# Three of four transposed attention tiles copied by ScalarE, with every engine's turn order redrawn

## What is computed

```python
x = x + L0_gnn(ln(x), adj)      # g0: three GRU steps over the adjacency
x = x + L0_ffn(ln(x))           # f0: eight experts, two chosen per node
x = x + L1_gnn(ln(x), adj)      # g1: one masked softmax attention
x = x + L1_ffn(ln(x))           # f1: attention over 64 slices, 8 heads
x = x + L2_gnn(ln(x), adj)      # g2: mean over neighbours
x = x + L2_ffn(ln(x))           # f2: a state-space block
x = x + L3_gnn(ln(x), adj)      # g3: two masked 4-head attention layers
x = x + L3_ffn(ln(x))           # f3: the upper half of the rows gets an FFN
```

```python
scores = einsum('bqhd,bkhd->bhqk', q, k) * scale
scores = where(adj_mask, scores, NEG_INF)
out = einsum('bhqk,bkhd->bqhd', softmax(scores), v)
```

## Time and profile before

| | us |
|---|---|
| three runs, median (lowest to highest) | 3333.42 (3329.63 to 3334.25) |
| the profiled execution | 3333.91 |
| its span, first to last instruction | 3332.1 |
| half 0, from its first transposes | 161.4 |
| a middle half | 198.9 |
| half 16 | 172.1 |

### The profile page before, as it was taken

One profiled execution on the slowest core, in us unless ns is written; L12 is line 12 of the kernel. 1 busy time (PEld: TensorE's weight loads), 2 busy tenths in 40 slices (PEclk: granted clock), 3 DMA queues, 4 the chain that ended last, 5 costly groups with the idle time before them and its releaser, 6 DMA issues.

```text
span 3332.1 us, 63179 instructions
## 1 busy us (share of the span) xinstructions
PE 3189.0 (96%) x25003; PEld 2274.5 (68%) x25020; DVE 2206.0 (66%) x6966; ACT 1787.1 (54%) x3341; POOL 629.6 (19%) x788
## 2 busy tenths in 40 slices
PE   8999999999999999999999999999999999999999
PEld 5766667666666766667666666766667666666677
DVE  3466767766676767667676666767667667666644
ACT  2347464564646547464564646557464654646433
POOL 0002112130221202112130221203112130211212
PEclk9999999999999999999999999999999999999989
DMA  3000000000000000000000000000000000000000
GB/s 136 1 7 1 20 4 17 7 1 20 5 17 7 1 23 1 20 4 17 7 1 23 1 17 7 1 23 1 20 4 17 7 1 20 1 7 1 4 5 5
DMA packets 28775, 40.72 MB, mean 12 GB/s; under 512 B 1344, under 2 KB 17728, under 8 KB 28224
## 3 DMA queue, kind: packets, MB, share of 16 engines
q1 hardware_dynamic: 28480, 36.67, 3.4%
HBM read 28.28 MB, written 4.19 MB: 10 GB/s over the span
## 4 chain that ended last, share of the span: by engine, by line
PE 73%; DVE 14%; ACT 9%; issue 3%; POOL 1%; DVEq 0%
PE ps L442 59%; ACT scratch L1066 6%; PE ps L901 6%; DVE scratch L1385 4%; DVE scratch L1379 3%; PE ps L451 2%; PE ps L1054 2%; DVE scratch L1888 1%; DVE scratch L1871 1%; POOL scratch L2097 1%; DVE scratch L1382 1%; ACT adjf L1066 1%; PE ps L614 1%; ACT xT L1066 1%; DVE x L1385 1%
## 5 line engine op out<-in xcount | busy, mean ns | idle before, releaser
L1066 ACT ACTIVATE scratch<-scratch 128x512 f32<-128x512 f32 (+4 forms) x832 | 567.6, 694 | 143.4 <-DVE scratch L1871 72.3
L442 PE MATMUL ps<-xT,weights_sb 128*128 128x512 f32 x1152 | 568.4, 603 | 7.3 <-ACT xT L1066 7.2
L442 PE MATMUL ps<-scratch 128*128 128x128 f32 (+6 forms) x4608 | 526.7, 378 | 26.0 <-ACT adjf L1066 6.6
L2097 POOL TENSOR_SCALAR scratch<-scratch 128x512 f32<-128x512 f32 x512 | 346.9, 695 | 985.1 <-DVE scratch L1878 985.1
L442 PE MATMUL ps<-weights_sb,scratch 128*128 128x128 f32 (+3 forms) x3840 | 491.8, 278 | 3.0 <-DVE scratch L1523 1.9
L442 PEld LDWEIGHTS ps<-weights_sb,scratch 128*128 128x128 f32 (+3 forms) x3840 | 440.7, 183 | 53.2 <-issue 39.5
L442 PEld LDWEIGHTS ps<-scratch 128*128 128x128 f32 (+5 forms) x4608 | 338.3, 159 | 125.7 <-issue 62.4
L1066 ACT ACTIVATE scratch<-ps 128x512 f32<-128x512 f32 (+2 forms) x384 | 212.2, 561 | 325.8 <-PE ps L442 212.2
L1871 DVE CUSTOM_DVE_ANT_0 scratch<-ps,nomask 128x512 f32<-128x512 f32 x512 | 334.4, 684 | 42.3 <-PE ps L442 41.3
L2080 POOL TENSOR_TENSOR rstd<-ve,minus_half 128x4 f32<-128x4 f32 x126 | 128.7, 1021 | 1223.6 <-DVE ve L1382 1222.0
L901 PE MATMUL ps<-weights_sb,scratch 128*128 128x128 f32 x2048 | 309.5, 278 | 29.9 <-ACT adjf L1066 7.8
(11 more groups left out here) (167 smaller groups left out, 4547.6 us busy)
## 6 DMA issues: line engine op xcount, KB each, us to landing
adj<-adj SPq DMA_DIRECT2D x16, 1024.0 KB, 5.7
weights_sb<-weights SPq DMA_DIRECT2D x1, 4605.0 KB, 19.4
x_in<-x SPq DMA_DIRECT2D x16, 256.0 KB, 2.7
scratch<-scratch SPq DMA_DIRECT2D x32, 128.0 KB, 2.3
out<-x SPq DMA_DIRECT2D x16, 256.0 KB, 2.5
scratch<-raw SPq DMA_DIRECT2D x1, 1645.0 KB, 21.9
weights_sb<-weights SPq DMA_DIRECT2D x1, 499.0 KB, 6.6
scratch<-raw SPq DMA_DIRECT2D x1, 384.0 KB, 5.1
```

The costliest lines, as they stand in the source:

```text
L442: return pe.matmul(o, lhsT, rhs, start=start, stop=stop, **k)
L1066: return act.activation(o, a, func, **k)
L2097: pool.tensor_scalar(p, p, cut(g, G3_RI + n, 1), 1.0, ALU.mult, ALU.mult).then_inc(s["att_p"], 1)
```

## The change

Of each query tile's four heads, head 0 still leaves ps7 by VectorE and heads 1, 2 and 3 now leave by ScalarE. The waits of PE on these copies, the semaphores' counts and the two engines' loops are changed to fit. The number of instructions of every other kind stays; all the strings of turns are new, and constant products stand at other places and in other numbers.

```diff
 SP_TURNS = (
-    "ellele"
+    "lleele"
 )
 ...
 PE_TURNS = (
-    "ee7777eeeeelelleleleelllllleeeeeeellll7777llllell7777777777777777777777777777777leellllllllleleeeeel"
+    "ee7777eeeeeeelllleleelllllleeeeeeellll7777llllell7777777777777777777777777777777lellelllllllleeeeeee"
 ...
-            "att_p": 2 * T * AH, "pT_psum": 2 * T * AH, "pT_dve": T * AH, "pT_act": T * AH, "pv_psum": 4, "h3_part": 4,
+            "att_p": 2 * T * AH, "pT_psum": 2 * T * AH, "pT_dve": 2 * T, "pT_act": 2 * T * (AH - 1), "pv_psum": 4, "h3_part": 4,
 ...
         def turned(layer, n, g):
-            return done("pT_act" if n % 2 else "pT_dve", g, (layer * T * AH + n) // 2)
+            if n % AH == 0:
+                return done("pT_dve", g, layer * T + n // AH)
+            return done("pT_act", g, (layer * T + n // AH) * (AH - 1) + n % AH - 1)
 ...
-                    pe.wait_ge(*turned(layer, AH * (2 * pair + 2) - 2, g))
+                    pe.wait_ge(*turned(layer, AH * (2 * pair + 1), g))
                     pe.wait_ge(*turned(layer, AH * (2 * pair + 2) - 1, g))
 ...
-                            if n > AH and n % 2:
+                            if n > AH and n % AH:
                                 yield from g3_turned(g, layer, n - AH)
 ...
                                 for h in range(1, AH):
                                     yield from g3_mask(g, layer, q * AH + h)
-                            if q:
-                                yield from g3_turned(g, layer, (q - 1) * AH + 2)
-                            if q < T:
                                 for p in range(2 * q, 2 * q + 2):
                                     yield from g3_sum(g, layer, p)
```

## The result

| | before | after |
|---|---|---|
| median (lowest to highest), us | 3333.84 (3329.63 to 3334.74) | 3403.63 (3398.32 to 3407.21) |
| the profiled execution and its span, us | 3333.91, 3332.1 | 3405.03, 3403.2 |
| a middle half, us | 198.9 | 203.2 in 7 of 15, 204.6 in 8 |

A forecast was written before the change was run, and what follows sets the result against it. PE was taken as the bound, so the effect is the change of its 27.9 us of waits a middle half: 1.9 - 0.4 - 0.4 = +1.1, times 15 is 16.5; 3333.9 + 16.5 - 2.9 = 3347.5 us, range 3314 to 3370.

The forecast's parts named there:

- step 4: Rest of a middle half: -0.4 us beside g0, g2 and f2, and -0.4 in the last part.
- step 3: f0 with layer 0 of g3: the new order costs +1.9 us a half, between +0.6 and +3.0.
- step 1: The moved copies: 590 ns on ScalarE against 685 on VectorE, at most 0.4 us a half, not counted apart.
- ScalarE's room: Up to layer 0's first values: two more copies take 1.2 of ScalarE's 3.8 us to spare.
- Turns 1 and 2: Start of layer 0: waits of 1.3 and 0.3 us plus 18 constant products of 1.2, together 2.8 us a half.
- What is given back: Layer 0 after the first values: more expert work covers turns 8 to 15, -1.1 us (0.3 to 1.8).
- idle time at the start: Start of f0's part: an expert's output moves ahead of g3's transposes and a 0.3 us wait goes.
- short waits: Layer 0 up to the first values: four waits of 0.1 to 0.2, together 0.5 us (0 to 1.2).
- rival (c): ScalarE late for all of layer 0: f0's part costs 3.0 us, a half 2.5; 3368.5 us, chance 0.10.
- Rival (b): Last part: f1 starts earlier beside layer 1 and fills waits, a half loses 1.2 us; 3313 us, chance 0.20.
- step 2: Constant products: +3.9 us in middle halves, -0.1 in half 0, -2.8 in half 16, together +1.0.
- over 62.5: Sign in the last part: if it takes over 62.5 us, turns 4 and 5 wait longer than thought.

The follow-up runs named there:

- experiment 1: The kernel before with its order kept and only head 2's copies moved to ScalarE: 3361.93 us, ratio 1.0088.
- experiment 5: The kernel of experiment 1 with tile 2 of layer 0 copied by VectorE again: 3336.39 us, ratio 1.001.
- experiment 6: The kernel of experiment 1 with ScalarE's copy of tile 2 of layer 0 one exponential later: 3351.13 us, ratio 1.005.
- experiment 13: The changed kernel with tile 1 of layer 0 copied ahead of tile 5's exponential and 12 constant products, not 18, ahead of turn 2: 3395.43 us, ratio 1.0193.
- experiment 10: The kernel of experiment 1 with the changed order only from g1's first transposes to ahead of turn 6 of layer 1: 3368.01 us, ratio 1.0105.
- experiment 12: The kernel of experiment 11 with the changed kernel's PE list for half 16 as well: 3332.04 us, ratio 0.9997.
- experiment 8: The changed kernel with 12 more constant products at f1's transposes in a middle half: 3398.01 us, ratio 1.019.
- experiment 11: The kernel before with its order kept and only tiles 2 and 6 of layer 1 copied by ScalarE: 3333.19 us, ratio 1.0001.
- experiment 2: The changed kernel's order on every engine, with head 2's tiles copied by VectorE as before: 3524.36 us, ratio 1.0575.
- experiment 9: The kernel of experiment 1 with the changed order only from ahead of turn 6 of layer 1 in the middle halves: 3375.42 us, ratio 1.0124.

## Why the prediction was wrong

Between the forecast's 13.6 us and the 71.1 of the profiles' spans lie 57.5. Of these, 32 are step 4 (25 of them the last part of the half), 16.5 are what step 3 gave back for layer 0, 11 are the clock, and half 16 takes off 2.6. By step:

- **The copies (step 1) and ScalarE's room (step 3).** The price of a copy was right (599 and 589 ns against 590). The step that failed as a reason reads "It gets two more copies there (tiles 2 and 6), 2 x 0.59 = 1.2 of its 3.8 us of room." Room over 28.6 us says nothing of one place. In the sum its 0.5 us held, for the changed order. Under the old order the copies cost 1.8 us a half, 1.5 of it by tile 2's copy alone (experiments 1, 5, 6). The changed order has no such wait at tile 2's copy; that its waits at turns 1 and 2 are the same price at another place was not shown, and the order costs another 1.5 us up to the end of layer 0.
- **Turns 1 and 2 (step 3).** 2.8 us were forecast and 2.70 are there, with the releasers and the 18 products as told. As a reason this was half right: where turn 2 came 0.5 us sooner, nothing was gained (experiment 13).
- **What is given back (step 3): the term that was mis-sized.** 1.1 us were taken off because more expert work is left for later turns. The trace of before has no idle time ahead of the first values that could have been filled, and of the idle time at turns 12 to 15 (0.48 us before) 0.25 went; the 12 constant products there all stayed, and PE's real products took 0.2 us more. The other small terms held: idle time at the start down 0.17 for 0.3, short waits 0.5 for 0.5. So the part came to +3.0 in place of +1.9, which is rival (c)'s price for it. (For a whole half that rival should have had 3.0 - 0.4 - 0.4 = 2.2, and 3364 us; its 2.5 doesn't follow from its terms.)
- **The rest of the half (step 4): the term with the wrong sign, and the largest.** -0.4 and -0.4 were read off the products' numbers, 8 fewer in each part. Idle time grew by 0.53 and by 1.48 instead, to +0.1 and +1.2. The forecast had said itself that "A product put in says that a wait is expected there, but not that it is all of the wait", and it then used the count as the measure all the same. What step 4 had wrong in the last part is turn 4 of layer 1. It names what is there, "turns 4 and 5 then find VectorE at g1's residual", and takes this as outweighed, -0.4. The whole +1.2 is lost ahead of turn 4, which in the changed kernel waits for the reciprocal behind that residual, by way of GpSimd's tile. Without that wait, PE's own order there would still cost 0.8 (7.70 for 6.92 in experiment 10).
- **Rival (b)'s mechanism is there and gave nothing.** f1's transposes come 27.2 us after g1's, where they came 32.9 after; but turn 15 of layer 1 comes at 47.6 in place of 41.3. From turn 4 to the end the half takes 54.10 us where it took 54.06: what was brought forward pushed back the other phase by as much.
- **Half 16 (step 2).** -2.8 was forecast and the profiles show -5.4, but that is no measurement of the list. Half 16 takes 172.1 and 168.3 us in two profiles with before's list (before, experiment 5) and 166.7, 168.2 and 169.8 in three with the changed one, and by experiment 12 the list gives 1.2 us in the medians, within the noise.
- **The clock: a term that was missing.** 8 x 1.4 = 11 us, which experiment 8 takes away.
- **The sum.** 15 x (0.1 + 3.0 + 1.25) + 11.2 - 5.4 = 71.1 us, the difference of the spans. The forecast's 13.6 were 15 x 1.1 - 2.9.

The text on the Trainium skill stood: Perfetto Trace Analysis, section Optimizing Scalar/DVE Operations, ties handing work to ScalarE to a saturated VectorE, and VectorE wasn't. The runs agree that there was nothing to gain (ratios 1.0088, 1.001 and 1.0001 in experiments 1, 5 and 11, under before's order). ScalarE wasn't saturated either (115.9 of 200.6 us), and still one copy of 0.60 us cost 1.5.

Of the signs that were named: the idle time over 1 us before turn 1, the 18 products, and idle time between the second scores and the first values are there. The part of f0 is 58.4 us and not 57.3, the last part is 63.15, which is the case "over 62.5", for which the prediction named turns 4 and 5, and the parts that should have been shorter are not.

What stays open: which wait sets the 1.5 us of the new order up to the end of layer 0 (experiment 13 rules out turn 2), and why the new order without its split is so much worse (experiment 2) beyond the row on GpSimd and the clock.

## What to carry to other kernels

An engine's spare time over a stretch is no price for work that is added to its queue: look at what stands behind the new instruction, and whether its input is there when the engine reaches it. One copy of 0.6 us that arrived a microsecond early cost more than seven others together. The same holds for a small instruction that another engine's chain begins with: a reciprocal of 0.16 us behind 3.5 us of other work held up GpSimd's tile and PE's transpose of it, by 1.59 us where nothing else was late (experiment 9). The number of filler products in a list measures the waits that its author could fill, not the waits; count idle time and fillers as one sum, and give back only what a row shows as idle or filled at the place that is to be covered.

## What the runs showed of the hardware

PE's granted clock fell to 0.50 for stretches of 3.4 us (some of 6.8) behind short waits, none over 0.56 us at f1's transposes. Where PE had been busy 2.44 of the 3.70 us ahead, the fall came in 8 of 15 alike halves and cost 1.4 us each time; where it had been busy 3.11, by 12 small products more, it came in none. Taking 18 such products out of a wait that they filled brought falls in six halves, 1.3 us for one of 3.4 us and 2.7 for the one of 6.8. Half 0, whose list was the same in six of the profiled kernels, took between 159.0 us (experiment 12, granted clock 0.96) and 165.5 us (experiment 6, 0.91) in them; so two kernels that differ by a few us are better compared by a middle half without a fall (198.9, 199.2, 200.0, 200.7) than by their medians.
